# A kernel for 32 head pairs of attention: the first pair's first maxima turned early, its first score tiles issued between later maxima, and the last pair's second sums taken on VectorE

## The reference

```python
xn = layernorm(x)                        # x: 4 batches x 1024 rows x 128
q, k, v = xn@Wq, xn@Wk, xn@Wv            # 16 heads of 64
w = softmax(q k^T / 64, causal)
mask = clip((key_index + span * 1024) / 33, 0, 1)    # per head and key
w = w * mask;  w = w / (sum(w) + 1e-8)
attn = (w v) @ Wo
x_dq = round(xn / scale) clipped to +-127, times scale
out = x + attn + x_dq @ (ternary - 1)^T + bias
```

## Time and profile before

| | us |
|---|---|
| median of 3 runs | 1007.33 (1005.56 to 1009.34) |
| the profiled execution | 1003.91 |
| its span | 1002.2 |
| TensorE busy | 981.3 (98%) |
| VectorE busy | 768.3 (77%) |
| GpSimd busy | 708.8 (71%) |
| ScalarE busy | 451.3 (45%) |

### The profile page before, as it was taken

How to read it: one execution, slowest core, us unless ns; L and a number is a source line. 1 busy time by engine, 2 the same in 40 slices (tenths; PEclk the granted TensorE clock), 3 DMA queues, 4 the chain that set the end, 5 groups by cost and what they waited for, 6 DMA issues and landing times.

```text
span 1002.2 us, 19150 instructions
## 1 busy us (share of the span) xinstructions
PE 981.3 (98%) x7081; PEld 631.0 (63%) x7081; DVE 768.3 (77%) x1734; ACT 451.3 (45%) x607; POOL 708.8 (71%) x650
## 2 busy tenths in 40 slices
...
DMA packets 16117, 8.52 MB, mean 9 GB/s; under 512 B 5388, under 2 KB 15628, under 8 KB 16024
## 3 DMA queue, kind: packets, MB, share of 16 engines
...
q10 hardware_dynamic: 608, 0.14, 0.1%
...
## 4 chain that ended last, share of the span: by engine, by line
PE 88%; DVE 8%; issue 2%; DMA 1%; ACT 1%; SPq 0%; DVEq 0%; ACTq 0%
PE ring L939 25%; PE pv L956 25%; PE ring L912 12%; PE beside L995 7%; PE beside L968 6%; PE ring L885 3%; PE ring L881 3%; PE ring L882 3%; DVE ring L732 2%; DVE v L718 2%; PE ring L899 1%; DVE beside L756 1%; PE beside L983 1%; PE beside L919 1%; PE ring L900 1%
## 5 line engine op out<-in xcount | busy, mean ns | idle before, releaser
L541 ACT ACTIVATE prob<-ring 128x1024 f32<-128x1024 f32 (+3 forms) x384 | 293.6, 810 | 348.2 <-PE ring L939 348.2
L475 POOL TENSOR_TENSOR psumd<-psumd,prob 128x512 f32<-128x512 f32 (+1 forms) x252 | 410.7, 1630 | 28.7 <-ACT prob L541 0.8
L732 DVE CUSTOM_DVE_ANT_0 ring<-ring,causal 128x128 f32<-128x128 f32 (+3 forms) x512 | 240.3, 517 | 96.4 <-PE ring L912 96.0
L939 PE MATMUL ring<-q,k 64*128 64x512 f32 (+3 forms) x2304 | 280.0, 347 | 3.9 <-DMA mrow<-maxrow 2.4
L956 PE MATMUL pv<-prob,v 128*64 128x512 f32 (+3 forms) x1536 | 267.2, 490 | 0.0
L448 POOL TENSOR_SCALAR_AFFINE_SELECT prob<-prob 128x256 f32<-128x256 f32 x256 | 107.0, 419 | 218.0 <-ACT prob L541 215.8
L939 PEld LDWEIGHTS ring<-q,k 64*128 64x128 f32 x2304 | 195.2, 185 | 39.4 <-DVE rowmax L732 5.7
L956 PEld LDWEIGHTS pv<-prob,v 128*64 128x64 f32 x1536 | 104.7, 137 | 153.6 <-issue 139.9
L736 DVE TENSOR_REDUCE rowmax<-ring 128x2 f32<-128x1024 f32 x128 | 151.4, 1222 | 4.7 <-PE ring L912 1.4
L471 POOL TENSOR_TENSOR psumd<-prob 128x768 f32<-128x768 f32 x64 | 134.8, 2106 | 23.1 <-ACT prob L541 18.3
L912 PE MATMUL ring<-k,q 64*128 64x512 f32 (+3 forms) x768 | 143.2, 408 | 5.4 <-ACT k L530 1.2
...
## 6 DMA issues: line engine op xcount, KB each, us to landing
...
kext<-kext SPq DMA_DIRECT2D x128, 4.0 KB, 1.7
...
mrow<-maxrow SPq DMA_DIRECT2D x64, 4.0 KB
...
```

The costliest lines, as they stand in the source:

```text
L475: g.tensor_tensor(acc[:, :, lo:HALF], acc[:, :, lo:HALF], pr[:, :, lo:HALF], ALU.add).then_inc(acc_done, 1)
L541: a.activation(prob[n % NPROB][:, :, lo:HALF], ring[:, slot(f"S{t}", i), :, lo:HALF], ACT.Exp, scale=1.0 / DH).then_inc(exp_done, 1)
L732: last = v.tensor_tensor_reduce(out=ring[:, s, h, 0:n], in0=ring[:, s, h, 0:n], in1=causal[:, HALF - n:HALF], scale=1.0, scalar=MASKED, op ...
L939: last = t_.matmul(ring[:, s, h, lo:HALF], k[p][rows, keys], q[p][rows, cols], start=(at == 0), stop=(at == len(parts) - 1))
```

## The change

At the beginning: the maxima `R0` to `R3`, which belong to query columns 0 to 511, are transposed on their own (`H`, two transposes to `beside`), copied by VectorE (`Hc`) into a corner of `lnden`, and put into `mrow` by two transfers that ScalarE issues (`Hrow`). SP's transfer for pair 0 then carries only the other columns. `S0` to `S3` of pair 0 wait for these rows and stand between `M7` and `Q` of pair 1; `T` comes after `K` of pair 1. The logarithms of the keys (`keys` on ScalarE) come ahead of the weights' high parts (`rest`); on GpSimd the clamp comes after half of the ramp instructions, and the low part of the logarithms ahead of the weights' low parts. `quantisation_scale` moves behind `Klo` of pair 1, and the first bias addition on GpSimd behind `Tc` of pair 0.

At the end: VectorE has a list for the last pair, `DVE_LAST`, with the additions `A5` to `A11`; GpSimd has only `A0` to `A3` there. `D1` reads the finished sum, and the eight direct matmuls are gone. `S6` moves ahead of `Y1` of pair 30, `S11` ahead of `Y0`, `D1` ahead of `F1` and `G7`.

```diff
-PE_FIRST = ("Q+ K+ M0+ M1+ M2+ I0+ M3+ I1+ M4+ I2+ M5+ I3+ M6+ I4+ M7+ I5+ M8+ M9+ M10+ M11+ Q++ T+ "
-            "K++ S0+ S1+ S2+ V+")
+PE_FIRST = ("Q+ K+ M0+ M1+ M2+ I0+ M3+ I1+ M4+ I2+ M5+ I3+ H+ M6+ I4+ M7+ I5+ S0+ M8+ M9+ S1+ M10+ S2+ "
+            "M11+ S3+ Q++ K++ T+ V+")
...
+POOL_LAST = "L0 A0 L1 A1 L2 A2 L3 A3 L8 L9 L10 L11"
+DVE_LAST = "Tc t1- u1- o1- Ya1- A5 A6 t0 u0 o0 A7 A8 A9 A10 A11 Ya0 t1 u1 o1 Ya1"
...
+                j0 = HB if i == 0 else 0
                 for h in range(2):
-                    sp.dma_start(mrow[p][h * DH:h * DH + 1, :].bitcast(F32),
-                                 maxrow[h * KB:(h + 1) * KB, :].bitcast(F32)).then_inc(mrow_landed[p], 16)
+                    sp.dma_start(mrow[p][h * DH:h * DH + 1, j0 * P:S].bitcast(F32),
+                                 maxrow[h * KB + j0:(h + 1) * KB, :].bitcast(F32)).then_inc(mrow_landed[p], 16)
...
+            ramp(0, H // 2)
             pool.wait_ge(w_lo_done, 2)
-            pool.wait_ge(key_step, 1 + H)
+            pool.wait_ge(key_step, 1 + H // 2)
+            pool.wait_ge(xn_done, KB)
             g.tensor_scalar(wgt, wgt, 0.0, 1.0, ALU.max, ALU.min).then_inc(wgt_done, 1)
             pool.wait_ge(wgt_done, 1)
+            ramp(H // 2, H)
...
+            pool.wait_ge(maxrow_done, 1)
             add_bias(0)
...
+                elif name == "Hrow":
+                    act.wait_ge(ext_done, 16 * NEXT)
+                    act.wait_ge(first_rows_done, 1)
+                    for h in range(2):
+                        act.dma_start(mrow[0][h * DH:h * DH + 1, 0:HALF].bitcast(F32),
+                                      first_rows[:, h * P:(h + 1) * P].bitcast(F32)).then_inc(first_rows_landed, 16)
...
+            def first_rows_out():
+
+                dve.wait_ge(first_rows_ready, 1)
+                v.tensor_copy(first_rows, beside[0:HB, 0:2 * P]).then_inc(first_rows_done, 1)
...
+            def add_last(t):
+
+                acc, before, pr = psumd[1], prob[(LAST * NT + t - 1) % NPROB], prob[(LAST * NT + t) % NPROB]
+                lo = first_col(t)
+                if is_diag(t):
+                    dve.wait_ge(sel_done, LAST * NDIAG + DIAG_UPTO[t])
+                else:
+                    dve.wait_ge(exp_done, tiles_upto(LAST, t))
+                if t == HB + 1:
+                    dve.wait_ge(den_ready, halves_upto(LAST - 1, 1))
+                    dve.wait_ge(acc_done, LAST * NT + HB)
+                    v.tensor_tensor(acc[:, :, lo:HALF], before[:, :, lo:HALF], pr[:, :, lo:HALF], ALU.add
+                                    ).then_inc(acc_done, 2)
+                else:
+                    dve.wait_ge(acc_done, LAST * NT + t)
+                    v.tensor_tensor(acc[:, :, lo:HALF], acc[:, :, lo:HALF], pr[:, :, lo:HALF], ALU.add
+                                    ).then_inc(acc_done, 1)
...
+            def turn_first_maxima():
+
+                pe.wait_ge(max_read, HB)
+                for h in range(2):
+                    last = t_.transpose(beside[0:HB, h * P:(h + 1) * P], rowmax[0][:, h * KB:h * KB + HB],
+                                        ident[:, :])
+                last.then_inc(first_rows_ready, 1)
...
-                direct = range(NT - HB, NT) if c == 1 and i == LAST else ()
-                pe.wait_ge(acc_done, tiles_upto(i, HB - 1 if c == 0 else NT - HB - 1 if direct else NT - 1))
+                pe.wait_ge(acc_done, tiles_upto(i, HB - 1 if c == 0 else NT - 1))
                 for h in range(2):
                     last = t_.matmul(out[h * DH:(h + 1) * DH, :], ones[:, :], psumd[c][:, h, :],
-                                     start=True, stop=not direct)
-                for t in direct:
-                    lo = first_col(t)
-                    pe.wait_ge(sel_done, i * NDIAG + DIAG_UPTO[t])
-                    for h in range(2):
-                        last = t_.matmul(out[h * DH:(h + 1) * DH, lo:HALF], ones[:, :],
-                                         prob[(i * NT + t) % NPROB][:, h, lo:HALF], start=False, stop=(t == NT - 1))
+                                     start=True, stop=True)
```

More of the change, by code:

```diff
@@ L41 @@
 POOL_PLAN = "L0 A0 L1 A1 L2 A2 L3 A3 A4 A5 A6 A7 L8 L9 L10 L11 A8 A9 A10 A11 B"
-PE_FIRST = ("Q+ K+ M0+ M1+ M2+ I0+ M3+ I1+ M4+ I2+ M5+ I3+ M6+ I4+ M7+ I5+ M8+ M9+ M10+ M11+ Q++ T+ "
-            "K++ S0+ S1+ S2+ V+")
-DVE_FIRST = ("Qlo+ Klo+ R0+ R1+ R2+ R3+ R4+ R5+ R6+ R7+ R8+ R9+ R10+ R11+ Rc+ Tc+ Qlo++ Klo++ keys+ Vs+")
-ACT_FIRST = "xf0+ Qhi+ xf1+ Khi+ rest+ keys+ wv+ Qhi++ Khi++ E0+ E1+ E2+"
-PE_LAST = "T G11- S0 S1 S2 D1- S3 S4 S5 Y1- S6 S7 D0 G3 S8 S9 S10 Y0 S11 F1 G7 D1 G11 Y1"
-POOL_LAST = "L0 A0 L1 A1 L2 A2 L3 A3 A4 A5 A6 L8 L9 L10 A7 L11"
+PE_FIRST = ("Q+ K+ M0+ M1+ M2+ I0+ M3+ I1+ M4+ I2+ M5+ I3+ H+ M6+ I4+ M7+ I5+ S0+ M8+ M9+ S1+ M10+ S2+ "
+            "M11+ S3+ Q++ K++ T+ V+")
+DVE_FIRST = ("Qlo+ Klo+ R0+ R1+ R2+ R3+ R4+ Hc+ R5+ R6+ R7+ R8+ R9+ R10+ R11+ Rc+ Tc+ Qlo++ Klo++ scale+ "
+             "keys+ Vs+")
+ACT_FIRST = "xf0+ Qhi+ xf1+ Khi+ keys+ rest+ Hrow+ wv+ E0+ E1+ E2+ E3+ Qhi++ Khi++"
+PE_LAST = "T G11- S0 S1 S2 D1- S3 S4 S5 S6 Y1- S7 D0 G3 S8 S9 S10 S11 Y0 D1 F1 G7 G11 Y1"
+POOL_LAST = "L0 A0 L1 A1 L2 A2 L3 A3 L8 L9 L10 L11"
+DVE_LAST = "Tc t1- u1- o1- Ya1- A5 A6 t0 u0 o0 A7 A8 A9 A10 A11 Ya0 t1 u1 o1 Ya1"
 SP_PLAN = "mrow kext+ store-"
@@ L103 @@
 IN_RING = [("X", -2)] + [u for u in PE_ORDER if u[0][0] in "QKSMV" or u == ("D1", LAST)]
-IN_BESIDE = [u for u in PE_ORDER if u[0][0] in "TDYXWF" and u not in (("D1", LAST), ("Y1", LAST))]
+IN_BESIDE = [u for u in PE_ORDER if u[0][0] in "THDYXWF" and u not in (("D1", LAST), ("Y1", LAST))]
 PLACE = {u: n for n, u in enumerate(IN_RING)}
@@ L257, in attention_ffn @@
         rowmax_done = sem("rowmax_done")
+        first_rows_ready = sem("first_rows_ready")
+        first_rows_done = sem("first_rows_done")
+        first_rows_landed = sem("first_rows_landed")
         maxrow_ready = sem("maxrow_ready")
```

30 lines of the change are left out of this document (22 added, 8 removed).

## The result

The changed kernel is **slower by 0.3%**: 1010.44 us median (1006.02 to 1011.96, 16 runs) against 1005.87 (1003.82 to 1009.34, 16 runs); ratio 1.0031, 95% interval 1.0015 to 1.0046. The ratio is near that of the means, 1009.6 to 1006.5; the medians lie 4.6 us apart, since five of the changed kernel's runs took only 1006 to 1007.2. I had forecast 1006.8, half a microsecond less than before, and a range from 1002.5 to 1009.5. The profiled execution has a span of 1008.4 us.

What follows compares the result with a forecast made beforehand. TensorE bounds the kernel, so its waits at both ends count: 1.1 us later at the beginning, 1.6 sooner at the end, -0.5 in all. Put on the three runs' median this gave 1006.8 us, range 1002.5 to 1009.5.

Steps and rivals of the forecast that it cites:

- second rival: Beginning: S0 holds the maxima up, by a late logarithm row (1.9 us) or halved clock (about 1 us); 1008.7 us, chance 0.23.
- beginning: Up to S4 of pair 0: S4 starts at 45.7 us instead of 44.62, 1.1 us later.
- end: Last pair: D1 at 987.5 us after VectorE's additions, last o at 995.2 instead of 996.83, 1.6 us sooner.
- What bounds: Middle thirty pairs: work and order unchanged, so only TensorE's waits at beginning and end count; a shift at S4 arrives in full.
- S0 at 26.6, held by the logarithms: Beginning: S0 starts at about 26.6 us instead of 35.29, waiting for the logarithms landing at 26.4.
- third rival: Beginning: S0 does not wait for the early rows (25.7 us) but the logarithms (26.4); alone moves nothing, no chance given.
- Pauses of VectorE ahead of R8 and R10: Beginning: VectorE loses 1.4 us ahead of R8 and 0.8 ahead of R10, as M8 and M10 stand behind S0 and S1.
- T behind Q and K costs: Beginning: T follows Q and K, 2.8 us of TensorE from 31.6 us on, so Tc ends at 35.1.
- The scale in the queue, 1.2: Beginning: the moved quantisation scale, formerly in a VectorE gap, queues ahead of Vs and costs 1.2 us.
- The meeting of VectorE and GpSimd at vtab, 1.6 us: Beginning: the vtab product waits for GpSimd's A1 until 41.3 us, so Vs ends at 42.8, not 41.2.
- the tenth that I allowed for its PSUM operand: End: lower bound on a full-width VectorE addition, a tenth below Vs's 1.23 us, since Vs reads PSUM.
- to waiting for A11: End: dropping the direct matmuls frees 2.15 us of TensorE, part of which goes to D1 waiting for A11.

Runs made afterwards that it cites:

- e5: The kernel before plus fourteen unread products where TensorE idled in the first 45 us, nothing of the change: 1004.41 us, ratio 0.9978.
- e10: The kernel before with only the change's beginning, plus unread products in TensorE's waits there: 1005.42 us, ratio 0.9989.
- e2: The kernel before with only the change's beginning, old end kept: 1010.31 us, ratio 1.0041.
- e12: e5 plus the change's end in its own order, with five unread products between Y0 and D1 of the last pair: 1002.77 us, ratio 0.9966.
- e1: The kernel before with only the change's end (VectorE additions, new order of the last pair): 1006.99 us, ratio 1.0008.
- e3: The changed kernel plus fourteen unread products where TensorE idled in the beginning: 1004.24 us, ratio 0.9979.
- e6: e2 with the quantisation scale put back ahead of all maxima: 1008.32 us, ratio 1.0024.
- e11: The changed kernel with M8 to M11 ahead of S0 to S3, scale in its old place, unread products, and G7 ahead of D1: 1000.17 us, ratio 0.9948.
- e4: e1 with G7 moved ahead of D1 in the last pair: 1001.26 us, ratio 0.9950.

## Why the prediction was wrong

**The step that failed** is the price of a wait on TensorE. I charged each wait at its own length. At one place I allowed that the granted clock falls behind a thin stretch and priced it at about 1 us, inside the second rival, with 0.23. The runs showed, against the kernel before (which loses 1.8 itself, 1006.2 less e5's 1004.4), some 3.5 us more than the sum at the beginning, and at the end 1.6 us more from T to `o`:

| us | forecast | with the waits filled | as it ran |
|---|---|---|---|
| beginning | +1.1 | +1.0 (e10 less e5) | +4.5 (e2 less before) |
| end | -1.6 | -1.6 (e12 less e5) | 0.0 from T to `o` (e1, and the changed kernel) |
| both | -0.5 | -0.6 | +4.6 between the medians, ratio 1.0031 |

The time of e1 says less about the end: +1.2 between the medians, with an interval from -1.0 to +2.6. The middle column is a sum of two experiments of another series than e5. The whole change with filled waits is e3, and its four runs at a clock of 1.0, 1002.1 to 1002.8, lie 1.6 to 2.3 below e5's median. Together with e10's runs at 0.999 this says that at full clock the new beginning costs about nothing. So the beginning's +1.0, close as it is to my +1.1, does not prove my sum.

Point by point:

- *What bounds.* Right for the middle: S4 to the last T stayed within 1 us. It is 919.6 to 919.7 in e3, e6, e10, e11 and e12, whose clock was whole behind S4, and 920.4 to 920.6 in the changed kernel, e1, e2 and e4, where S4 itself ran at half clock; the others lie between 919.5 and 919.9.
- *S0 at 26.6, held by the logarithms.* 27.93 with an input that came 0.9 later, so 0.4 late. Right. The third rival, that the early rows are not what it waits for, holds by the row above; when those rows landed the profile does not show.
- *Pauses of VectorE ahead of R8 and R10.* Both there. Their sizes, 2.3 and 1.6 for 1.4 and 0.8, are those of a slow clock; at full clock, in e10, they are 1.76 and 0.84. `Rc` at 0.17 us: right in kind.
- *T behind Q and K costs.* Right in e10, where they ran at full clock (2.1 us of idle VectorE). In the changed kernel Q and K, 2.8 us of TensorE in my sum, took 4.5.
- *The scale in the queue, 1.2.* Measured 1.1 (e6).
- *The meeting of VectorE and GpSimd at vtab, 1.6 us.* Did not happen, in any profile. In the changed kernel the product took 0.29 us and started as GpSimd's addition did, which then took 1.95 instead of 1.81. By the Trainium skill (SBUF — State Buffer, section SBUF: two separate sides) whichever starts first gets the ports for the whole instruction, and the other fully blocks. The trace agrees for `Rc` and for the selects at the end. It does not in e6 and e11, where GpSimd's copy started 0.18 and 0.19 us ahead of the product: that took 0.37 and 0.35 us and was over before the copy. In e6:

```profile
42.80 0.86 POOL L486 TENSOR_SCALAR psumd<-prob 128x256 f32<-128x256 f32 x1 [0.16 <-POOL prob L465]
42.98 0.37 DVE L723 TENSOR_TENSOR vtab<-mask,wrec 128x128 f32<-128x128 f32 x1
```

  Without this term my own sum has S4 0.5 us sooner, not 1.1 later; e10's median is 1.0 up, and its runs at 0.999 are level with e5's. That the forecast for the beginning came near e10's median is luck: a term that was not there stood in for others that I did not have (the slow first Q and K of that profile, the unread products themselves, pauses 0.4 us longer in sum). How the 1.0 us divides among these is not shown.
- *The end.* Every step to `D1` right. The additions took 1.23 us in full width, as long as `Vs`, so the tenth that I allowed for its PSUM operand is not there. What I named as freed TensorE time going "to waiting for A11" is what cost the end its gain, and I had it in hand: a 2 us wait near the end of a kernel whose trace showed a clock of 0.50 behind another thin stretch.
- *The scatter.* I took the 3.8 us between the three runs for noise and widened the range by it. It was the signal: among the runs of the kernel before, the time follows the granted clock, and the profiled execution, which I noted as 3.4 below the median, was one of the good ones. A sum made on it leaves out what the others lose. With 16 runs the median before is 1005.87, not the 1007.33 that the forecast started from.

The second rival, slower, had the right sign and place, and as one reason the clock; its 1008.7 was too low since it counted one price or the other, and left the end alone.
